# Half-precision planes for the feed-forward input and shared weights, and routing weights normalised after the gather

## What is computed

```python
def ffn(x):                       # N = 2048 tokens, D = 256, E = 64, K = 4, F = 64
    logits = flat @ router_w.T
    scores = softmax(logits)
    topk_idx = top_k(logits + router_bias, 4)
    topk_w = take(scores, topk_idx); topk_w = topk_w / topk_w.sum(-1)
    # 32 slots per expert: tok_table, w_table
    xg = flat[tok_table]
    y = (silu(xg @ gate_w.T) * (xg @ up_w.T)) @ down_w.T
    out = zeros.at[tok_table].add(y * w_table)
    out += (silu(flat @ sh_gate.T) * (flat @ sh_up.T)) @ sh_down.T   # 512 hidden
x = x + 0.5 * ffn(layernorm(x))
x = x + attention(layernorm(x))   # 16 heads of 128, weights codes * scales
x = x + 0.5 * ffn(layernorm(x))
```

## Time and profile before

| | us |
|---|---|
| timed runs | 968.83, 971.72, 972.66 |
| median | 971.72 |
| profiled execution, its span (its own time isn't given apart from it) | 969.0 |
| TensorE busy in the span | 918.5 |
| VectorE, ScalarE, POOL busy | 764.3, 647.1, 645.5 |

### The profile page before, as it was taken

One profiled execution on the slowest core, in us unless ns is written; L12 is line 12 of the kernel. 1 busy time (PEld: TensorE's weight loads), 2 busy tenths in 40 slices (PEclk: granted clock), 3 DMA queues, 4 the chain that ended last, 5 costly groups with the idle time before them and its releaser, 6 DMA issues.

```text
span 969.0 us, 18581 instructions
## 1 busy us (share of the span) xinstructions
PE 918.5 (95%) x5809; PEld 559.7 (58%) x5812; DVE 764.3 (79%) x2079; ACT 647.1 (67%) x1426; POOL 645.5 (67%) x607
## 2 busy tenths in 40 slices
PE   7989888999999999999999999999999999977987
PEld 4766465555555555555555555555555555765666
DVE  6954399998888888888888888888878789876247
ACT  5624546887777687777778778777777787643431
POOL 3367778878576868778676766867677455336642
PEclk9999999999999999999999999999999999989999
DMA  8979745566766878797885755756675574485657
GB/s 335 367 243 314 265 170 164 108 132 113 144 132 104 157 158 186 153 211 162 175 192 98 154 107 133 153 104 138 108 153 93 93 117 91 80 334 170 244 204 274
DMA packets 302978, 165.58 MB, mean 171 GB/s; under 512 B 278176, under 2 KB 285600, under 8 KB 300832
## 3 DMA queue, kind: packets, MB, share of 16 engines
q1 hardware_dynamic: 297696, 146.56, 62.8%
q0 software_dynamic: 3072, 9.44, 3.0%
q10 hardware_dynamic: 2112, 8.39, 2.2%
HBM read 68.93 MB, written 28.31 MB: 100 GB/s over the span
## 4 chain that ended last, share of the span: by engine, by line
PE 75%; DVE 13%; issue 4%; DMA 3%; ACT 3%; POOL 1%; SPq 0%; another core or an unknown queue 0%; ACTq 0%; DVEq 0%; POOLq 0%
PE b_o L110 5%; PE b_o L112 5%; PE b_o L111 5%; PE b_p L110 5%; PE b_s L110 5%; PE b_s L112 5%; PE b_s L111 5%; PE b_p L111 5%; PE b_p L112 5%; PE b_out L110 3%; PE b_out L112 3%; PE b_out L111 3%; PE b_v L110 2%; PE b_v L112 2%; PE b_v L111 2%
## 5 line engine op out<-in xcount | busy, mean ns | idle before, releaser
L2460 POOL TENSOR_TENSOR h<-pr,h 128x512 f16<-128x512 f32 x256 | 293.0, 1157 | 159.9 <-ACT h L1179 154.2
L1169 ACT ACTIVATE pr<-b_s,nmax,kappa 128x512 f32<-128x512 f32 x256 | 197.6, 774 | 42.2 <-DVE nmax L1915 37.0
L1912 DVE TENSOR_SCALAR_CACHE_REDUCE junk<-b_s 128x512 bf16<-128x512 f32 x256 | 175.3, 685 | 22.6 <-PE b_s L112 17.5
L1179 ACT ACTIVATE h<-pr 128x512 f16<-128x512 f32 x256 | 153.2, 626 | 0.8 <-DMA pT<-h 0.4
L1943 DVE SCALAR_TENSOR_TENSOR x<-b_out,rinv,x 128x256 f32<-128x256 f32 x256 | 111.4, 476 | 41.7 <-PE b_out L112 40.2
L110 PE MATMUL b_p<-xh,w 128*128 128x512 f16 x256 | 97.0, 379 | 4.3 <-DVE qT L1854 2.6
L110 PE MATMUL b_o<-pT,v 128*128 128x512 f16 x256 | 97.0, 379 | 1.7 <-DVE oT L1931 1.7
L110 PE MATMUL b_s<-kT,qT 128*128 128x512 f16 x256 | 97.0, 379 | 0.7 <-ACT pr L1169 0.7
L112 PE MATMUL b_s<-kT,qT 128*128 128x512 f16 x256 | 97.0, 379 | 0.0
L111 PE MATMUL b_s<-kT,qT 128*128 128x512 f16 x256 | 97.0, 379 | 0.0
L111 PE MATMUL b_o<-pT,v 128*128 128x512 f16 x256 | 97.0, 379 | 0.0
(11 more groups left out here) (225 smaller groups left out, 2236.6 us busy)
## 6 DMA issues: line engine op xcount, KB each, us to landing
raw<-in_experts SPq DMA_DIRECT2D x32, 768.0 KB, 7.2
raw_cs<-in_heads SPq DMA_DIRECT2D x16, 1024.0 KB, 5.1
zrows<-zero ACTq DMA_DIRECT2D x4, 2048.0 KB, 11.6
z<-zrows SPq DMA_DIRECT2D x16, 512.0 KB, 4.2
zrows<-zero SPq DMA_DIRECT2D x16, 512.0 KB, 4.0
zl<-zrows SPq DMA_DIRECT2D x16, 512.0 KB, 10.5
rows<-xn SPq DMA_DIRECT2D x8, 512.0 KB, 12.1
pT<-h SPq DMA_TRANSPOSE x256, 3.2
```

Source lines behind the costliest of these rows:

```text
L1169: act.activation(pr[n % 4][:], b_s[n % 3][:], ACT.Exp, bias=nmax[:, u % 2, i:i + 1], scale=kappa[:, s:s + 1], accum_out=rsum[:, u % 2, i:i ...
L1179: act.activation(h[n % 4][:, 0, :], pr[n % 4][:], ACT.Copy).then_inc(q["p_high"], 1)
L1912: dve.tensor_scalar(junk[n % 2][:], b_s[n % 3][:], 0.0, None, ALU.add, ALU.max, accum_out=peaks[:, n % 2:n % 2 + 1]).then_inc(q["peak_read ...
L2460: pool.tensor_tensor(h[n % 4][:, 1, :], pr[n % 4][:], h[n % 4][:, 0, :], ALU.subtract).then_inc(q["p_split"], 1)
```

## The change

- x, router, gate and up are held in two float16 planes; xT is gone, and the FFN reads xh as attention does, x scaled by 2. Down stays fp32r.
- float16 needs a range, so router, gate and up get a power-of-two scale each. `squares_shared(j)` (ScalarE) squares and sums, `norm_shared(j)` (TensorE) adds over the partitions, `scales_shared(j)` (VectorE) forms scale and undo factor; `job` and `low_job` apply the scale, `silu`, `hidden` and `logits_out` the undo factor.
- The low plane of down moves from VectorE (`low_job(3)`) to POOL (`low_down`).
- `sum_weights` and `weighted` are gone. Unnormalised weights are stored right after `masked`; `slot_weights` sums the 64 weights of each gathered row as well, takes the reciprocal and multiplies.
- All five lists have a new order, mostly before unit 8 and after unit 56 of attention. SP loads router and gate ahead of x(2) and up, and issues store_rows between the loads; ScalarE issues the four zeroing writes after `logits_out(3)` instead of from `high(1)` on; output(63, 0) and output(63, 1) come before router(10) and gate_up(18).

```diff
-            xT.append(m.keep(f"xT{k}", [P, DC, N], F32R))
+        xh = [m.keep(f"xh{k}", [P, DC, N], F16) for k in range(2)]
-        rw = m.keep("rw", [P, DC, 2 * E], F32R)
+        rw = m.keep("rw", [P, DC, 2 * E], F16)
-        gw = [m.keep(f"gw{k}", [P, DC, SH], F32R) for k in range(2)]
-        uw = [m.keep(f"uw{k}", [P, DC, SH], F32R) for k in range(2)]
+        gw = [m.keep(f"gw{k}", [P, DC, SH], F16) for k in range(2)]
+        uw = [m.keep(f"uw{k}", [P, DC, SH], F16) for k in range(2)]
...
+            def norm_shared(j):
+                pe.wait_ge(q["in_squared"], j + 1)
+                pe.wait_ge(q["consts"], 3)
+                pe.matmul(shared_norm(j), ones[:], sh_norms[:, j:j + 1], start=True, stop=True).then_inc(q["in_normed"], 1)
...
             keep_busy(0, 22)
+            norm_shared(0)
             turn(0)
+            norm_shared(1)
+            norm_shared(2)
             keep_busy(1, 15)
+            keep_busy(2, 3)
             router(0)
-            keep_busy(2, 3)
+            turn(1)
             logits(0)
-            turn(1)
             gate_up(0)
...
             probs_values(63, 3)
             turn(10)
+            output(63, 0)
+            output(63, 1)
+            router(10)
             gate_up(18)
-            output(63, 0)
-            router(10)
-            output(63, 1)
+            logits(10)
             gate_up(19)
-            logits(10)
+            turn(11)
             gate_up(20)
-            turn(11)
             router(11)
...
+            def squares_shared(j):
+                src, _, sem = shared[j]
                 act.wait_ge(q[sem], 16)
+                act.activation(square_w[j][:], src.rearrange("p c f -> p (c f)"), ACT.Square, scale=float(P // 8),
+                               accum_out=sh_norms[:, j:j + 1]).then_inc(q["in_squared"], 1)
...
+            squares_shared(0)
+            squares_shared(1)
+            normalise(0)
+            squares_shared(2)
+            high(0)
             job(0)
-            normalise(0)
             job(1)
-            high(0)
+            job(2)
             normalise(1)
             logits_out(0)
-            job(2)
+            high(1)
             normalise(2)
-            high(1)
-            zero_out(0)
-            job(3)
             normalise(3)
...
+            def scales_shared(j):
+                dve.wait_ge(q["in_normed"], j + 1)
+                own.did(dve.tensor_single_scalar(sh_halves[:, j:j + 1], shared_norm(j).bitcast(I32), ZBITS + 1,
+                                                 ALU.arith_shift_right))
+                own.wait()
+                own.did(dve.tensor_scalar(sh_undo[:, j:j + 1], sh_halves[:, j:j + 1], float(2 ** ZBITS), 50.0 * 2 ** ZBITS, ALU.mult,
+                                          ALU.add))
+                own.wait()
+                dve.tensor_scalar(sh_scale[:, j:j + 1], sh_halves[:, j:j + 1], -float(2 ** ZBITS), 203.0 * 2 ** ZBITS, ALU.mult,
+                                  ALU.add).then_inc(q["sh_scaled"], 1)
...
-                dve.tensor_tensor(hid[n % 2][:], up[bank_of(n)][:], sil[n % 2][:], ALU.mult).then_inc(q["hid_ready"], 1)
+                dve.scalar_tensor_tensor(out=hid[n % 2][:], in0=up[bank_of(n)][:], scalar=power_of(sh_undo, 2), in1=sil[n % 2][:],
+                                         op0=ALU.mult, op1=ALU.mult).then_inc(q["hid_ready"], 1)
...
-            def sum_weights(lap):
-                dve.wait_ge(q["masked"], lap + 1)
-                own.did(dve.tensor_reduce(esum[:], ex[:], X, ALU.add))
-                own.wait()
-                dve.reciprocal(rsum_w[:], esum[:]).then_inc(q["sum_ready"], 1)
...
                 own.did(dve.tensor_tensor(wtmp[s][:], xg[G % XGS][:, D:ROW], sel[:, 60 - EG * g:60 - EG * g + E], ALU.mult))
+                own.did(dve.tensor_reduce(whole[:, g:g + 1], xg[G % XGS][:, D:ROW], X, ALU.add))
                 own.wait()
-                dve.tensor_reduce(ws[:, g:g + 1], wtmp[s][:], X, ALU.add).then_inc(q["ws_ready"], 1)
+                own.did(dve.tensor_reduce(part[:, g:g + 1], wtmp[s][:], X, ALU.add))
+                own.did(dve.reciprocal(fraction[:, g:g + 1], whole[:, g:g + 1]))
+                own.wait()
+                dve.tensor_scalar(ws[:, g:g + 1], part[:, g:g + 1], fraction[:, g:g + 1], None, ALU.mult).then_inc(q["ws_ready"], 1)
...
             first_keys(2)
-            sum_weights(0)
+            first_keys(3)
             hidden(4)
-            first_keys(3)
             hidden(5)
...
+            def low_down():
+                src, (hi, lo), _ = shared[3]
+                pool.wait_ge(q["p_hi"], 4)
+                pool.tensor_tensor(lo, src[:], f32(hi), ALU.subtract).then_inc(q["hlo_done"], 1)
```

More of the change, by code:

```diff
@@ L615, in _ @@
             gate_up(1)
+            router(3)
             logits(2)
-            router(3)
+            logits(3)
             gate_up(2)
-            logits(3)
             gate_up(3)
@@ L2130, in _ @@
             maxima(6, 3)
-            maxima(7, 0)
+            outputs(4)
             add(3, 1)
             sums(5)
+            maxima(7, 0)
             values(7)
@@ L2212, in _ @@
-            maxima(60, 3)
+            maxima(61, 0)
+            maxima(61, 1)
             values(60)
-            maxima(61, 0)
             keys_of(62)
-            maxima(61, 1)
+            outputs(58)
             queries(62)
-            outputs(58)
             add(57, 1)
+            statistics(8)
             maxima(61, 2)
+            maxima(61, 3)
+            maxima(62, 0)
+            add(58, 0)
+            values(61)
             sums(60)
-            values(61)
-            statistics(8)
@@ L2261, in _ @@
             hidden(16)
+            route(9)
             hidden(17)
-            route(9)
+            outputs(63)
             add(62, 1)
-            outputs(63)
             low(10)
@@ L2766, in _ @@
             scatter(28)
+            hidden_low(25)
             scatter(29)
```

1019 lines of the change are left out of this document (507 added, 512 removed).

## The result

The changed kernel took 982.42 us (median of 4 runs, 981.38 to 982.92), the kernel before 971.29 in the same series; the ratio is 1.0118, 95% interval 1.0103 to 1.0132. The forecast of 963.0 was wrong by 19.4 us, the time lies outside its range of 956 to 972, and the chance of 0.69 had been given to "faster".

A forecast was written before the change was run, and what follows sets the result against it. Bound by a front latency chain, TensorE in expert stages and VectorE up to attention, likewise in the second FFN. Sum: -3.2 +0.5 -2.5 -1.4 +0.9 -3.0 = -8.7 us; 971.7 - 8.7 = 963.0 us, range 956 to 972.

The forecast's parts named there:

- What bounds the kernel: Whole kernel: latency chain in front, TensorE's queue in expert stages, VectorE up to attention; attention full, moving only as a block.
- Part 1: Router, gate and up matmuls in half-precision planes: 7.1 us less TensorE time, 3.2 us gained, bounds 0.6 and 7.1.
- rival C: Gate, up and router matmuls: fp16 brings TensorE nothing; 966.2 us, chance 0.05.
- Part 2: Scales and the new start: 0.5 us lost, bounds a gain of 1 and a loss of 3.
- Part 3: Normalisation moved to the gathered row, shorter routing chain and earlier store: 2.5 us gained in front, 1.4 in the rear.
- rival D: First gather: another semaphore (rows or zeroing) holds it despite the weights' edit; +1.1, 964.1 us, chance 0.05.
- Part 4: Three more VectorE instructions per group in slot_weights, mostly hidden: 0.9 us lost, bounds 0 and 14.7.
- Rival B: Expert stages: slot_weights becomes the link, each exposed group paying 0.44 us; up to 976.8 us, chance 0.08.
- Part 5: Attention's end, outputs first: earlier statistics and router(11) at the high clock; 3.0 us gained, bounds 4.2 gain, 0.5 loss.
- rival A: Attention's end: no gain, VectorE holds the last addition and the clock falls anyway; 966.0 or 968.5 us, chance 0.30.
- Other swaps: Remaining reorderings (turn_expert, outputs, maxima by a place or two): attention stays full, so nothing, bounds 1 either way.

The follow-up runs named there:

- d_order_cheap: c_before_order with the gathered row's weight in two VectorE instructions again, division by the sum left out; 969.68 us against 977.08, ratio 0.9996 to the kernel before.
- c_before_order: Changed kernel's operations and new start, everything behind in the old queue order, zeroing writes apart again; 977.08 us, 1.0054 of the kernel before.
- b_after: The changed kernel, unchanged, on a slower chip; 999.82 us, 0.9993 of the kernel before there.
- b_attention: Changed kernel with only the operations of attention's units 0 to 8 back in the old order, slower chip; 993.87 us, 0.9938 of the kernel before.
- c_after: The changed kernel, unchanged, measured and profiled again on a faster chip; 983.02 us, 1.0139 of the kernel before.
- c_both: Changed kernel with attention's first eight units and GpSimd's queue from gather(16) on in the old order; 975.73 us, 1.0037 of the kernel before.
- e_both_cheap: c_both with the gathered row's weight in two VectorE instructions, division by the sum left out; 973.15 us against 975.73.

## Why the prediction was wrong, point by point

**What bounds the kernel** was read rightly for the middle of attention, and wrongly in one sentence: "attention stays full, so nothing". It is full only where the loop runs. Its first eight units are written by hand, and there a swap by three places can put a load ahead of the transposes for which TensorE waits.

**Part 1** (3.2 gained). The pace was right: the first gate matmul starts at 19.16, the next at 19.38, and later ones 0.216 apart, against the earlier trace rows; rival C fell. The path was not. The kernel before, then d_order_cheap, in front of attention and behind it:

```profile
0.00:141.20 141.20, 118.59 (x920) 84.10 (x923) 89.88 (x271) 68.14 (x161) 84.30 (x90) 0.99 0.79 287
845.90:969.00 123.10, 104.14 (x859) 78.45 (x859) 72.05 (x183) 42.68 (x103) 56.22 (x50) 0.96 0.68 244
```

```profile
0.00:141.00 141.00, 117.04 (x929) 66.75 (x930) 88.13 (x277) 71.75 (x167) 84.73 (x90) 0.99 0.79 287
845.20:968.00 122.80, 102.69 (x860) 64.04 (x858) 71.81 (x181) 43.92 (x103) 53.68 (x49) 0.95 0.69 245
```

TensorE's busy time falls by 1.5 us in each, the stretches only by 0.2 and 0.4. Share of the chain is not what a microsecond is worth: TensorE's busy time turned into idle time. Waits for what, is mixed: those for `hid` fell in front from 6.8 to 5.5 us and rose behind from 2.2 to 2.8. By medians all edits but the three instructions brought 0.8 us (970.5 to 969.7), within what can be told from nothing.

**Part 2** (0.5 lost) erred on the safe side. gate_up(0) started at 19.16, not 21.3 to 23.3, and the last mask was 1 to 3 us early.

**Part 3** (2.5 in front, 1.4 in the rear). The chain did get shorter: indices at 57.26 in the old order. But gather(0) came earlier than 61.09 in no kernel with the writes ahead of the store. The prediction saw this ("the store shares the DMA engines with them; if it took 8 us") and took 8 for the worst; it took 10.3, and rival D, which comes nearest to this, got 0.05. In the changed kernel itself the indices were no earlier either (61.26), for the turned mask came late. In the rear keys to indices fell from 15.8 to 14.7 us, 1.1 instead of 1.4, in the new order, and not at all in the old one (15.9).

**Part 4** (0.9 lost, bounds 0 and 14.7) is the largest miss among the edits: 7.4 us in the old order; in the new one 2.6 by medians, which is within the spread. It used VectorE's mean load, 8.0 of 20 us, as cover. A mean says nothing of a short link: `ehid` of the next group stands behind the batch, and TensorE waits for it. Nor was it asked what a VectorE instruction with two SBUF operands meets on GpSimd. Rival B had the mechanism, with a chance of 0.08 as it asked for all of it.

**Part 5** (3.0 gained). The clock came as forecast; router(11) and logits(11) in the changed kernel, to hold against 2.09 and 1.97 us in the earlier trace rows:

```profile
863.58 1.03 PE L369 MATMUL rl<-xh,rw 128*128 128x512 f16 x4
865.38 1.10 PE L378 MATMUL rl<-pick,lgT 128*128 128x64 f32 x8 [0.78 <-ACT lgT L1120]
```

That is 1.9 us. Not all of it is the order's: in c_before_order, with the old one, router(11) took 1.04 us too, and only logits(11) 1.97, as in every kernel with the old rear. The wait of 2.25 us ahead of router(11) is gone in the new order. The earlier statistics did not come: from the last x to router(11) 10.8 us, before 10.4, as rival A says, whose other half, that the clock falls all the same, was wrong. Together with Part 3, last x to gather(16) fell by 2.8 us; 4.4 were forecast.

**What the sum left out.** "Other swaps ... have no price that a row shows; attention stays full, so nothing, bounds 1 either way." This is the step that failed by most: the swaps in attention's first eight units cost 6.0 us on a slower chip (b_after to b_attention) and, with GpSimd's part, 7.3 on a faster one (c_after to c_both). By medians on the faster chips: 12.4 us lost = 7.3 for attention's order (GpSimd's part included) + 2.6 for the weights + about 2.5 in which the gains of Parts 2, 3 and 5, the bunched zeroing writes and the rest cancel. No run took these 2.5 apart, the 2.6 may be nothing, and each median is uncertain by some microseconds. The gains of 8.7 us net that the sum expected did not come: c_both and e_both_cheap are 5.1 and 2.2 us above the kernel before.

## What to carry to other kernels

Where a diff reorders hand-written queues, walk each one for a newly placed instruction that waits for a DMA or works long ahead of a producer of the critical engine; the price is in what stands behind it, and a range of 1 us is not earned by having found no row. Slack is read per link: ask what is queued behind the lengthened instruction, not how busy its engine is on average. A transfer that is issued earlier lands earlier only if fewer bytes are ahead of it, and a stage difference from one profile is to be seen in a second one before a theory is built on it. When a product waits for a transfer, look at what stood ahead of that transfer in its own queue, and not only at the engine that made its data.

## What the runs showed of the hardware

- Of four 2 MB writes issued in a row on ScalarE's queue the fourth issue took 6.68 us (6.5 to 6.7 in c_after, c_both and b_after), where the others took 0.57 to 0.77 us, and ScalarE's computing instructions waited.
- A transpose's issue on SyncE's queue, 1.2 to 1.4 us in nine of ten cases, took 3.85 us behind a load of 1 MB, to within 0.02 us of the load's landing.
- A store of 512 KB landed in 4.1 to 4.3 us with no zeroing write ahead of it or only one that was about to land, and in 10.1 to 13.0 us behind 2 MB writes from another queue.
- A VectorE product of two SBUF tiles of 128x64 took 4.14, 3.13 and 2.16 us instead of 0.22, each time up to the end, within 0.1 us, of GpSimd instructions that ran beside it; of the products over 0.6 us 39 of 40 did so, within 0.12 us.
- After 3.35 us without a matmul the granted clock was low in the changed kernel's profile (0.59 from 43.2 to 50 us); after 3.65 us at the same place it was 1.00 in c_both's.
- The same kernel took 971 us on some chips and 1001 on others; attention ran at the same pace (526.9 and 527.0 us), the expert stages 10 to 18 us longer, with idle stretches of 1.9 to 2.7 us on ScalarE that nothing in the profile explains.
